# Flamingo gated block: up chunk of the gated FFN inside the last attention batch, last residual tiles copied by ScalarE and added by GpSimd

## What is computed

```python
# attention of layer 1, input1 = layernorm(x), input2 = ctx_2048
theta_x = einsum('ld,bdt->btl', theta_w, input2) + theta_b
phi_x = einsum('ld,bdt->blt', phi_w, input1) + phi_b[:, None]
p = softmax(einsum('btl,bls->bts', theta_x, phi_x), axis=-1)
g_x = einsum('ld,bdt->btl', g_w, input1) + g_b
t_x = einsum('bts,bsl->blt', p, g_x)
h = relu((t_x - mean) * rsqrt(var + LN_EPS) * ln_gamma + ln_beta)   # over latent and time
w_t = einsum('ol,blt->bot', out_w, h) + out_b[None, :, None]
x = x + tanh(g_xattn[1]) * (w_t + input2)
# gated FFN of layer 1, on layernorm(x): linear_bit = rmsnorm, 8 bit rows, ternary weights
h = silu(linear_bit(x, w1, g1)) * linear_bit(x, w2, g2)
x = x + tanh(g_ffn[1]) * linear_bit(h, w3, g3)
```

## Time and profile before

| | before |
|---|---|
| timed runs, median | 635.82 us (635.71, 637.44, 635.82) |
| profiled execution, its own time | 637.47 us |
| span in the profile, first to last instruction | 635.7 us |
| granted TensorE clock, mean | 0.997 |
| TensorE matmul busy | 608.2 us, 96% |
| VectorE, ScalarE, GpSimd busy | 542.8, 474.3, 352.3 us |

### The profile page before, as it was taken

How to read it: one execution, slowest core, us unless ns; L and a number is a source line. 1 busy time by engine, 2 the same in 40 slices (tenths; PEclk the granted TensorE clock), 3 DMA queues, 4 the chain that set the end, 5 groups by cost and what they waited for, 6 DMA issues and landing times.

```text
span 635.7 us, 9329 instructions
## 1 busy us (share of the span) xinstructions
PE 608.2 (96%) x2775; PEld 359.6 (57%) x2804; DVE 542.8 (85%) x1066; ACT 474.3 (75%) x716; POOL 352.3 (55%) x432
## 2 busy tenths in 40 slices
PE   6899999999999999989999999999788999999996
PEld 6777777777777444444445565555333444444443
DVE  3697888889999889876779988899898999999864
ACT  3469785765764899987763487667689999999984
POOL 2589888888877454310000111114488989889861
PEclk9899999999999999999999999999999999999999
DMA  8959896799999689739359900000116666566651
GB/s 301 379 196 309 291 331 230 251 326 338 340 306 317 258 274 305 183 90 358 140 108 197 249 26 16 16 17 17 51 46 170 182 167 181 165 187 171 181 154 50
DMA packets 141989, 125.20 MB, mean 197 GB/s; under 512 B 96048, under 2 KB 104000, under 8 KB 140800
## 3 DMA queue, kind: packets, MB, share of 16 engines
q1 hardware_dynamic: 134512, 110.52, 57.4%
q10 hardware_dynamic: 7440, 14.24, 6.7%
HBM read 68.04 MB, written 33.64 MB: 160 GB/s over the span
## 4 chain that ended last, share of the span: by engine, by line
PE 67%; DVE 13%; ACT 10%; issue 5%; DMA 2%; POOL 2%; SPq 0%; ACTq 0%; DVEq 0%; POOLq 0%
PE ps L1226 22%; PE ps L1506 14%; PE ps L1522 8%; PE ps L1344 7%; ACT turn L1015 4%; PE ps L1433 3%; PE ps L1463 3%; PE ps L1481 2%; PE ps L1437 2%; PE ps L1235 2%; PE ps L1413 1%; PE ps L1423 1%; DMA arena<-kpad_d 1%; DVE turn L1899 1%; ACT arena L968 1%
## 5 line engine op out<-in xcount | busy, mean ns | idle before, releaser
L1226 PE MATMUL ps<-arena 128*128 128x288 f32 x640 | 160.8, 408 | 4.3 <-DMA arena<-kpad_d 2.8
L1226 PEld LDWEIGHTS ps<-arena 128*128 128x128 f32 x640 | 119.6, 190 | 36.2 <-issue 3.4
L1506 PE MATMUL ps<-arena 128*128 128x512 bf16 x510 | 113.4, 379 | 4.1 <-DVE arena L2094 4.0
L1506 PEld LDWEIGHTS ps<-arena 128*128 128x128 bf16 x512 | 49.5, 98 | 66.0 <-DVE arena L2094 3.2
L737 POOL TENSOR_TENSOR arena<-arena 128x512 f32<-128x512 f32 x64 | 80.3, 1275 | 8.9 <-DVE arena L2094 7.9
L621 POOL TENSOR_TENSOR arena<-arena 128x1024 f32<-128x1024 f32 x32 | 60.6, 1893 | 17.9 <-issue 11.3
L1522 PE MATMUL ps<-arena 128*128 128x512 bf16 x241 | 57.1, 379 | 1.9 <-ACT arena L1129 0.7
L1375 PE MATMUL ps<-arena 128*128 128x512 bf16 x251 | 55.3, 379 | 1.2 <-DVE arena L1843 0.9
L1344 PE MATMUL ps<-arena 128*128 128x512 bf16 (+1 forms) x249 | 55.4, 379 | 0.6 <-ACT arena L968 0.3
L628 POOL TENSOR_TENSOR turn<-turn 128x512 f32<-128x512 f32 x31 | 40.5, 1306 | 22.8 <-DVE turn L1678 22.8
L2094 DVE SCALAR_TENSOR_TENSOR arena<-ps,up_scale,arena 128x512 f32<-128x512 f32 x64 | 46.7, 745 | 5.8 <-ACT arena L1105 5.0
(11 more groups left out here) (232 smaller groups left out, 1281.0 us busy)
## 6 DMA issues: line engine op xcount, KB each, us to landing
arena<-in_L_ffn_w SPq DMA_DIRECT2D x48, 512.0 KB, 6.1
arena<-kpad_d ACTq DMA_DIRECT2D x16, 512.0 KB, 7.1
hq_d<-arena SPq DMA_DIRECT2D x14, 512.0 KB, 2.7
tern_d<-late SPq DMA_DIRECT2D x24, 256.0 KB, 5.4
arena<-in_ctx SPq DMA_DIRECT2D x4, 1024.0 KB, 11.4
arena<-in_L_ffn_w ACTq DMA_DIRECT2D x8, 512.0 KB, 5.8
arena<-in_ctx SPq DMA_DIRECT2D x2, 2048.0 KB, 10.6
x_d<-arena SPq DMA_DIRECT2D x4, 1024.0 KB, 5.3
```

Of the source, the lines that this page charges most:

```text
L1226: last = pe.matmul(ps[:, 4 * s + lo, 0:NB * PAIRS], toep[:, u, (LB - 1 - lo + li) * P:(LB - lo + li) * P], kv[:, s, li, :], start=(li == 0 ...
L1506: last = pe.matmul(ps[:, bank, :], xq4T[:, s, 4 * j + k, :], w[:, k, c * L:(c + 1) * L], start=(k == 0), stop=(k == LB - 1))
```

## The change

In attention batch 7, TensorE does chunk 0 of up(0) in banks 0 and 1 (`up_banks` returns them) between the turned probabilities and their product, waiting for x3_done = 6 + 12, and chunk 1 after the product. out_proj(6) moves behind latent_mean(7) and waits for gate(0,0,0). Chunks 2 and 3 follow it, then out_proj(7), which waits for the copies of out_proj(6). ScalarE loads Silu's table ahead of its copies in batch 7 and does silu(0,0,0) at the batch's end. attn_end(6) and attn_end(7) are gone from VectorE; ScalarE's `x3_copy(b)` copies each projected bank with its bias column into a slot of `xo`, in columns 512 to 2559 of turn, and counts x3_done. GpSimd's `x3_add(r)` adds slot r to tile 12 + r of x_res, after its ffn_body(1), (2), (3) and (4). VectorE does gate(0,0,0) in batch 6, ahead of x_stats(2), and gate(0,0,1) ahead of x_max(2); before tile 6 (and each fourth after it) it waits for the four additions.

```diff
+        xo = turn[:, L:5 * L].rearrange("p (r l) -> p r l", r=4)
@@ up_banks
+            if isinstance(t, int) and t == 0 and c == 0:
+                return 0, 1
@@ GpSimd
-            ffn_body(1, 1, True)
-            with po.loop(NT // 2 - 2, 2 * 5) as i:
+            def x3_add(r):
+                pool.wait_ge(S["x3_done"], 6 + 2 * NB - 4 + r + 1)
+                x = x_res[:, NT - 4 + r, :]
+                pool.tensor_tensor(x, xo[:, r, :], x, ALU.add).then_inc(S["xb_added"], 1)
+
+            for t in range(1, 5):
+                ffn_body(t, t % 2, True)
+                x3_add(t - 1)
+            ffn_body(5, 1, True)
+            with po.loop(NT // 2 - 4, 2 * 5) as i:
                 for u in range(2):
-                    ffn_body(2 * i + 2 + u, u, True)
+                    ffn_body(2 * i + 6 + u, u, True)
@@ ScalarE, attn_body
+                if not nxt:
+                    act.activation(junk[:, 0:1], eps_ln[:, 0:1], ACT.Silu)
                 for k in range(4):
                     act.wait_ge(S["pt_tr"], 4 * b + k + 1)
...
                 else:
                     relu(b - 1)
+                    silu(0, 0, 0)
+
+            def x3_copy(b):
+                for o in range(2):
+                    act.wait_ge(S["wt_done"], 2 * b + o + 1)
+                    act.activation(xo[:, 2 * (b - NB + 2) + o, :], ps[:, o, :], ACT.Identity,
+                                   bias=cols3[:, 2 + o:3 + o]).then_inc(S["x3_done"], 1)
@@ ScalarE, ffn_body
-                silu(t, s, 0)
+                if prev:
+                    silu(t, s, 0)
                 if late and t == 1:
                     x_centre(t + 2)
+                silu(t, s, 1)
                 if not prev:
+                    x3_copy(NB - 2)
                     relu(NB - 1)
-                silu(t, s, 1)
+                if late and t == 1:
+                    x3_copy(NB - 1)
...
-            act.activation(junk[:, 0:1], eps_ln[:, 0:1], ACT.Silu)
@@ TensorE, attn_body
                 if not nxt:
+                    pe.wait_ge(S["bw_ready"], 12)
+                    pe.wait_ge(xT_in[0], 16)
+                    pe.wait_ge(S["th_out"], NB)
+                    pe.wait_ge(S["x3_done"], 6 + 2 * NB - 4)
+                    up(0, 0, range(1))
                     pe.wait_ge(S["ln_ready"], b)
...
-                if not nxt:
-                    out_proj(b - 1, NB)
@@ TensorE, after the attention
+            up(0, 0, range(1, 2))
             latent_mean(NB - 1)
-            pe.wait_ge(S["bw_ready"], 12)
-            pe.wait_ge(xT_in[0], 16)
-            up(0, 0, range(4))
+            pe.wait_ge(S["h_done"], 3)
+            out_proj(NB - 2, NB)
+            up(0, 0, range(2, 4))
+            pe.wait_ge(S["x3_done"], 6 + 2 * NB - 2)
             out_proj(NB - 1, NB)
@@ VectorE
                     x_scales(1, 1)
+                    gate(0, 0, 0)
                     x_stats(2)
                 if late and b == NB - 1:
-                    attn_end(b - 1)
                     latent_ln(b)
...
-            gate(0, 0, 0)
+            gate(0, 0, 1)
             x_max(2)
-            gate(0, 0, 1)
             x_scales(2, 2)
...
             gate(1, 1, 1)
-            attn_end(NB - 1)
             gate(1, 1, 2)
...
                 for u in range(4):
+                    if u == 3:
+                        v.wait_ge(S["xb_added"], NT + 4)
                     ffn_body(4 * i + 3 + u, (3 + u) % 4, True, True, True)
```

More of the change, by code:

```diff
@@ L1079, in attn_body, with silu @@
                     relu(b - 1)
+                    silu(0, 0, 0)
[4 more added lines that the diff above has]
+                                   bias=cols3[:, 2 + o:3 + o]).then_inc(S["x3_done"], 1)
+            def silu(t, s, c):
+                act.wait_ge(S["upa_done"], 4 * t + c + 1)
+                act.activation(sil[:, c, :], ps[:, up_banks(t, c)[0], :], ACT.Silu,
+                               scale=up_scale[:, s, 0:1]).then_inc(S["sil_done"], 1)
             def x_quant(t):
@@ L1101, in x_centre @@
                                bias=mv[:, 0, 0:1]).then_inc(S["xc_ready"], 1)
[L1103 to L1106, removed]
             def h_quant(t, s, n):
@@ L1481, in out_proj @@
                     pe.matmul(ps[:, o, :], wT3[:, 6 + o, :], hln[2], start=True, stop=True).then_inc(S["wt_done"], 1)
[L1483 to L1489, removed]
             def up(t, s, chunks):
@@ L1494, in up @@
                     if isinstance(t, int) and t < 2:
-                        if 4 * t + c >= 2:
+                        if 4 * t + c >= 3:
                             pe.wait_ge(S["h_done"], 4 * t + c + 1)
@@ L1508, in up @@
                         last.then_inc(S[done], 1)
+            project(0, 0)
+            scores(0, 0)
+            attn_body(0, 0, True, False)
+            with pe.Fori(0, NB // 2 - 1) as i:
+                for u in range(2):
+                    attn_body(2 * i + 1 + u, (1 + u) % 2, True, True)
+            attn_body(NB - 1, 1, False, True)
             def hidden_T(t, n, parts, bank):
@@ L2038, in x_widen, with gate @@
                 v.tensor_copy(qb4, qi4).then_inc(S["qb_ready"], 1)
+            def gate(t, s, c):
+                v.wait_ge(S["sil_done"], 4 * t + c + 1)
+                v.wait_ge(S["upb_done"], 4 * t + c + 1)
+                v.scalar_tensor_tensor(out=hh[:, s % 2, c * L:(c + 1) * L], in0=ps[:, up_banks(t, c)[1], :],
+                                       scalar=up_scale[:, s, 1:2], in1=sil[:, c, :],
+                                       op0=ALU.mult, op1=ALU.mult).then_inc(S["h_done"], 1)
             def attn_body(b, p, nxt, nxt2, prev):
@@ L2088, in _ @@
             attn_body(NB - 1, 1, False, False, True)
[L2091 to L2096, removed]
             def h_max(t, s, n):
```

## The result

| | before | after |
|---|---|---|
| timed runs of this comparison, median | 637.31 us (20 runs, 635.66 to 638.83) | 639.23 us (20 runs, 637.79 to 640.37) |
| ratio, 95% interval | | 1.003 [1.0022, 1.0038] |
| profiled execution, its own time | 637.47 us | 639.32 us |
| its span | 635.7 us | 637.3 us |

The change costs 1.9 us (1.4 to 2.4): 0.3% slower, at the bound of what was called telling. Forecast were +1.2 us and 637.0. The kernel before came out at 637.31 over 20 runs, while the prediction started from a median of three, 635.82. That base alone is 1.5 of the 2.2 us by which 637.0 was too low; the other 0.7 belongs to the change. The ratios in this document leave out executions more than 1.5% above the fastest of their kernel, of which there is one, of 1308.89 us, in e4_batch7_vectorE.

A forecast was written before the change was run, and what follows sets the result against it. TensorE was taken to bound the FFN, and a VectorE and ScalarE chain the passage before up(3). Passage -0.8 plus additions +2.0 gave +1.2 us, on the median 635.82: 637.0 us, range 635.0 to 638.4.

The forecast's parts named there:

- The base: Whole kernel: the summed difference of +1.2 us was applied to the timed median of 635.82 us, giving 637.0.
- Passage, -0.8: Attention batch 7's scores to the first matmul of up(3): a shorter VectorE and ScalarE chain starts up(3,0) 0.8 us earlier.
- The four marks: Passage times forecast: up(3,0) 486.3, L1973 458.5 released by GpSimd, x_scales(2) 461.0, h_quant(0) 469.5.
- at the same sum: VectorE ahead of x_scales(2): gate(0,1) and x_max(2) swap with unchanged total; gate(0,0) already done gives 0.66 us.
- Additions, +2.0: GpSimd in FFN tiles 2 to 4: three exposed additions make TensorE lose 2.0 us over up(4) to up(6).
- The slack at TensorE: Gates ahead of up(4) to up(6): 0.13 us at up(4), taken as 0.2, subtracted from GpSimd's lag of 2.17.
- The room is used in full: GpSimd's pauses in tiles 2 to 4: the additions use all of that room, and not more.
- Each 1.24: GpSimd's exposed additions: each takes 1.24 us, so three ask 3.72 us.
- the room of 1.55 us: GpSimd's pauses at L744 in tiles 2, 3 and 4, less starts: 0.48 + 0.60 + 0.47 us to absorb additions.
- Hidden additions: Rival, FFN tiles: GpSimd's delay stays off TensorE, time 635.0 us; chance 0.15.
- a passage that returns nothing or very much: Two rivals on the passage: returns nothing, 637.8 us, chance 0.09; TensorE's idle shrinks by 4 or more, 633.8, chance 0.04.
- The port collision: Rival: VectorE's cast blocks GpSimd behind each exposed addition, 0.42 us more, 1.66 each; 638.3 us; chance 0.20.

The follow-up runs named there:

- e4_batch7_vectorE: Changed kernel with attn_end(7) back on VectorE and only batch 6's two additions on GpSimd, both at waits; ratio to before 0.9984 [0.9972, 0.9995].
- e7_batch6_alone: Kernel before, with only batch 6's two tiles copied by ScalarE and added by GpSimd in hidden places; ratio to before 0.9983 [0.9959, 1.0008].
- e10: Changed kernel with the cast x_widen of tiles 4 to 15 on 2 of 1024 columns; ratio to before 1.0025 [1.0011, 1.0038].
- e2: Changed kernel with each GpSimd addition on 256 of its 512 columns; ratio to before 0.9997 [0.9985, 1.0009].
- e1: Changed kernel without GpSimd's four additions and VectorE's wait for them, ScalarE still copying; ratio to before 0.9981 [0.997, 0.9992].
- e6: Changed kernel with the additions of tiles 2, 3 and 4 ahead of h_gain(t,3) instead of behind it; ratio to before 1.0121 [1.0104, 1.0138].
- e5: e4_batch7_vectorE with x_max(2) put ahead of latent_ln(7)'s last step, in VectorE's wait for GpSimd; 635.63 us, ratio to before 0.998 [0.9969, 0.9991].

## Why the prediction was right or wrong, point by point

**The base.** The difference was applied to a median of three runs, two at 635.7 to 635.8 and one at 637.4. The profiled execution, at 637.47, had the span that the sum was made on, 635.7; 637.47 + 1.2 = 638.7 would have stood within 0.6 us of the result. This step failed by 1.5 us, and by it the time fell outside the range. The rest of the miss is the additions' term, 1.0 too small, and the passage, 0.14 too large; against them stands the shorter end of the kernel, 0.5 us in the two traces, which the forecast did not have and which fits the timed difference (1.9) being smaller than the one at TensorE (2.36).

**Passage, -0.8.** Right in kind, a little too large: -0.66. The four marks have to be read with the 0.25 us by which everything is earlier from upstream: up(3,0), forecast for 486.3, stands at 486.20, in the time of before 486.45; L1973 (L2002 in the kernel after), forecast for 458.5, at 458.55 and released by GpSimd as said; x_scales(2), forecast for 461.0, at 461.20; h_quant(0), forecast for 469.5, at 469.70. So attn_end(6), behind gate(0,0)'s new place, gave 0.11 for 0.15, by the mechanism named (alone it gives 0.41, e7_batch6_alone), and the step that failed by 0.2 is the next one: gate(0,0) out of the chain, and x_max(2) and gate(0,1) changing places "at the same sum". x_scales(2) starts 1.32 us after x_max(2), while gate(0,1) between them had hidden the end of that operation. The table load, the copies and attn_end(7) cost nothing, as forecast; e4 and the fence of ScalarE show it.

**Additions, +2.0.** The form was right: pauses used up, VectorE waiting for GpSimd's power, TensorE short of gates ahead of three tiles and never again. The term was mis-sized, 2.98. L747 (L744 in the earlier trace rows), counted from up(3,0), lags by 1.08, 2.03 and 3.33 us, where 0.76, 1.40 and 2.17 were forecast. The slack at TensorE, taken as 0.2, was between 0 and 0.35: up(4), up(5) and up(6) start 0.86, 2.03 and 2.98 us late. The 1.16 us that the lag is too long are 0.73 of the meeting with the cast (e10), 0.32 of GpSimd's new wait for gate(4,3) at 508.97, and about 0.1 in the starts. "The room is used in full" was right (e2, and the missing pauses). "Each 1.24" missed the meeting. And the room of 1.55 us was some 0.3 too large: the wait for gate(4,3) isn't a consequence of TensorE running late, as e1 has it with no addition and TensorE on time (0.33), and there it eats into the third pause, 0.30 instead of 0.54. It comes from the unexplained delay of x_stats(7), and in e1 it goes with a loss of 0.14 us at TensorE.

**The rivals.** Hidden additions fell (the row of e1 against that of after), and so did a passage that returns nothing or very much (-0.66). The port collision came at all three additions, but at 0.24 us each, not 0.42, because L744 would have ended at 488.80 without the cast and ends at 489.05 with it, just behind the cast's end at 489.00: only the rest of the cast counts, not its 0.42 us. So its mechanism was right and its price half; its total of +2.4 us over the kernel before (638.2 on the base of 635.8, where 638.3 is given) is nearest to the trace's +2.32, though it left out GpSimd's wait. It should have been a term of the forecast, not a rival: that the cast would start just as the addition ends had been worked out, and it did. The Trainium skill, "SBUF — State Buffer", section "Who interferes with whom", says that, when VectorE runs in a two-port mode beside GpSimd, whoever issues first has the shared ports for the whole instruction and the other blocks fully. The trace agrees on both sides: L744 goes from 0.19 to 0.44 us behind a cast, and in e6 the cast goes from 0.42 to 2.53 us behind a GpSimd operation of 2.35.

## What to carry to other kernels

In a ring of engines whose bound is busy all the time, a pause of 0.5 us takes in 0.5 us of a 1.24 us operation once; the rest arrives in full at the bound, is never regained, and spacing the operations out does not help: place them where a wait is about as long as they are or longer, as e4 does (waits of 1.02 and 1.74 us for operations of 1.24). Before moving work next to a cast on VectorE, write down which of the two starts first, before and after the move, since 0.1 us in the order decided over 2.1 us. And take a small forecast as a difference between two profiles, on a base of more than three runs.

## What was not expected of the hardware

**The cast that waits.** A cast of 0.42 us took 2.53, 2.54 and 2.59 us in e6, each started 0.04 to 0.1 us behind a GpSimd x_gain of 2.35; in e5 one took 1.40.

**Two levels of time.** Both kernels take one of two times, about 1.5 us apart: in the kernel after, spans of 635.8 to 636.6 us come with a mean granted clock of 1.000 (with one exception at 637.1) and spans of 637.1 to 638.4 with 0.997. Busy time by stretches, from 19 to 23 us, in the kernel before (0.997):

```profile
19.00:23.00 4.00, 4.00 (x20) 3.67 (x20) 1.50 (x4) 2.73 (x5) 2.03 (x4) 0.57 1.07 390
```

and in e1_no_adds (1.000):

```profile
19.00:23.00 4.00, 4.00 (x29) 3.44 (x29) 3.04 (x6) 3.25 (x5) 2.08 (x4) 1.00 1.06 388
```

In the first the granted clock is 0.57 over these 4 us, that is mostly the lower level, 1.2 GHz, and 20 matmuls are done in place of 29. It comes after TensorE had been without work from 15.0 to 17.8 us, in some executions and not in others of the same kernel. It lies some 420 us ahead of the change. It is why three runs are a poor base here, and why absolute times of two traces differ by up to 1.9 us at the mean's matmul: 443.70 to 444.00 in the five traces with a mean clock of 1.000, 445.07 to 445.60 in the seven with 0.996 or 0.997.
